# Identity products in TensorE's rests, a convolution that starts before the last stores have landed, and weight splits spread over it: one decoder layer on one core

## The chip, the cores and the metric

The kernel runs on one core of a Trainium2 chip. A core has five engines with queues of their own: TensorE (PE, the matrix products; PEld is its loading of the stationary operand), VectorE (DVE), ScalarE (ACT), GpSimd (POOL) and SyncE (SP, which here issues all the DMAs). They meet by semaphores. The metric is the time of one execution on the device in microseconds (us); lower is better.

## The reference

One layer of a decoder on 16 sequences of 512 tokens with 256 features, all in fp32. Three parts, each followed by a residual sum and a layernorm:

```python
x = _layernorm(x + _L0_attn_ref(x, ...))      # a gated long convolution, then a gated MLP of 672
x = _layernorm(x + _L0_xattn_ref(x, ctx_512, ...))   # causal attention, 16 heads, plus attention to 64 context rows
x = _layernorm(x + _L0_ffn_ref(x, ...))       # low-rank MLP 256 -> 64 -> 1024 -> 64 -> 256 with GELU

# in _L0_attn_ref:
z = rmsnorm(u, pre_norm_w) @ in_proj_w.T                # 768 channels
z_pre = conv_general_dilated(zc, short_w, ...) + short_b[None, :, None]      # 3 taps per channel
x2, x1, v = jnp.split(z_pre, 3, axis=1)
h = jnp.sum(residues[:, :, None] * jnp.exp(log_poles * t[None, None, :]), axis=1)
xv = x1 * v
yconv = irfft(rfft(xv, n=n) * rfft(h, n=n)[None], n=n)[..., :Lc]    # causal convolution, 512 long
y = (yconv + xv * D_skip[None, :, None]) * x2
y = y.transpose(0, 2, 1) @ out_proj_w.T + u
zm = rmsnorm(y, post_norm_w)
return y + jax.nn.gelu(zm @ l1_w.T) * (zm @ l2_w.T) @ l3_w.T
```

## The kernel before

The program is five stages, each a `Block` in which every engine has its own list. A block ends with a barrier of all engines, so the next stage's first instruction on any engine comes after the last of this one on every engine. Loops over the 16 sequences (`over`, `over_late`) write out the first and last steps and loop over the rest.

- **project** (`pj_` tiles, lines 230 to 526): per sequence, rmsnorm, transpose on TensorE (`turn`, L452), six products of 128 channels (`products3`, L125 to L127), the taps on ScalarE and VectorE. SyncE's `store` writes the gate `x2` to memory (`gate_d`, L284) when tap 0 is done and then the chunks of `xv` into the resident tile `xv_all` (L287) when they are transposed. At the end SyncE waits for all these stores; then a second small block (`Names.clear`, L102 to L108) clears the stage's 28 semaphores.
- **longconv** (`lv_`, 529 to 671): the convolution by chunks of 32, as a scan over chunk states. 32 pairs of channel groups, all written out. Per pair GpSimd builds three small filter tiles, TensorE runs `gather` for the pair after next (L613), the products inside a chunk (L627) and those that leave a state (L634); VectorE scans the states (L663), and ScalarE copies the result back into `xv_all` (L582, L585). TensorE's products of a pair wait until ScalarE has copied the pair before last. In the pairs of the table `WEIGHTS` ScalarE also makes the rounded high halves of the MLP's five weights (`weight_high`) and VectorE, a pair later, the low halves (`weight_low`).
- **mlp** (`ml_`, 674 to 1030): per sequence the output projection (`out_product`), rmsnorm, transpose (`turn`, L932), gate and up products, GELU, the down product (`down`). A product in fp32 precision is made of three products of rounded halves, so `products3` is the unit everywhere.
- **attend** (`at_`, 1096 to 1734): a hand-written table of slots (`SLOTS`) fixes for each engine which job stands where. Jobs t0 and t1 transpose x, q and k project queries and keys, whose parts go to memory and back (`parts_d`), y and p at the end transpose and project the result. The first two steps (b = -2 and -1) only fill the pipeline, and `TAIL` empties it.
- **ffn** (`ff_`, 1758 to 2025): `turn` (L1828), `first`, `hidden` (L1842, L1843), `second` (L1850), `last_product`.

## Time and profile before

| | us |
|---|---|
| runs | 2195.28, 2195.38, 2197.44 |
| median | 2195.38 |
| the profiled execution | 2197.36, of which 2195.6 span |
| TensorE busy | 1985.4 (90% of the span) |
| VectorE, ScalarE, GpSimd busy | 1468.2, 1222.3, 883.2 |
| mean granted clock of TensorE | 0.965 |

The stages lie one behind another in the span: project until 217, longconv until 287, mlp until 784, attend until 1977, ffn to the end. The granted clock is given as a share of 2.4 GHz; it has two levels, 1.00 and 0.50 (1.2 GHz), and a value between is a mean over a stretch with both. A row of the timeline gives the start, the duration and the count of instructions that follow each other, and in brackets how long the engine had been idle and which engine's work ended that.

### The profile page before, as it was taken

What the parts mean: (1) busy time and instruction counts of PE and PEld (TensorE: products, weight loads), DVE (VectorE), ACT (ScalarE), POOL (GpSimd) and SP (SyncE); (2) the same over time, 40 slices, a digit from 0 to 9 for tenths busy, and PEclk for the clock granted to TensorE, in tenths of its full rate; (3) what the DMA queues carried; (4) which work ended last, traced back from release to release, by engine and by line L of the source; (5) the groups of instructions that cost most, each with busy time, mean ns of one, the idle gap of its engine ahead of it and who ended that gap; (6) DMA issues with size and microseconds to landing.
All of it is one profiled execution on the core that took longest, in us unless ns stands there. A gap on an engine that the chain in (4) does not pass through costs nothing. (4 is left out here: it accounts for less than half of the span.)

```text
span 2195.6 us, 39396 instructions
## 1 busy us (share of the span) xinstructions
PE 1985.4 (90%) x12897; PEld 1348.4 (61%) x12960; DVE 1468.2 (67%) x2652; ACT 1222.3 (56%) x2425; POOL 883.2 (40%) x1336
## 2 busy tenths in 40 slices
PE   6786949999999868999999999999999999968997
PEld 4665337888888755566566665566655665535554
DVE  6898634555555427777778777777777787724776
ACT  6775535555555423665656656565656556645554
POOL 3443615555555431334333434344333433332222
PEclk9999969999999979999999999999999999978999
DMA  3343121211122244343443344342443334112221
GB/s 116 123 149 125 44 77 68 77 68 69 67 73 76 78 106 91 77 106 72 104 105 85 79 93 103 92 103 64 109 103 80 90 81 94 43 39 66 78 87 66
DMA packets 104787, 188.10 MB, mean 86 GB/s; under 512 B 27961, under 2 KB 78137, under 8 KB 98489
## 3 DMA queue, kind: packets, MB, share of 16 engines
q1 hardware_dynamic: 104632, 186.13, 31.7%
q8 instruction: 86, 1.41, 0.3%
q14 instruction: 69, 0.56, 0.1%
HBM read 110.23 MB, written 58.79 MB: 77 GB/s over the span
## 5 line engine op out<-in xcount | busy, mean ns | idle before, releaser
L1516 ACT ACTIVATE at_pt<-at_ps_w 128x512 f32<-128x512 f32 x640 | 377.8, 598 | 232.8 <-PE at_ps_w L1392 232.7
L1743 DVE TENSOR_REDUCE at_mneg<-at_ps_s 128x1 f32<-128x384 f32 (+3 forms) x704 | 437.3, 636 | 94.9 <-PE at_ps_s L1381 87.3
L1606 POOL TENSOR_SCALAR_AFFINE_SELECT at_pt<-at_pt 128x256 f32<-128x256 f32 (+1 forms) x640 | 233.5, 368 | 576.3 <-ACT at_pt L1516 573.8
L1380 PE MATMUL at_ps_s<-at_ks,at_qs 96*128 96x128 bf16 (+3 forms) x1024 | 259.4, 306 | 25.0 <-DVE at_mneg L1743 22.7
L1392 PE MATMUL at_ps_w<-at_qs,at_ks 97*128 97x512 bf16 (+3 forms) x1024 | 244.3, 301 | 9.0 <-ACT at_pt L1516 5.0
L1380 PEld LDWEIGHTS at_ps_s<-at_ks,at_qs 96*128 96x128 bf16 x1024 | 86.2, 99 | 215.1 <-DVE at_mneg L1743 140.5
L895 POOL TENSOR_TENSOR ml_m_lo<-ml_m,ml_m_hi 128x512 fp32r<-128x512 f32 x80 | 115.9, 1450 | 181.0 <-ACT ml_m_hi L801 180.7
L1408 PE MATMUL at_ps_o<-at_pt,at_val 128*32 128x512 f32 (+3 forms) x2048 | 169.1, 449 | 9.7 <-POOL at_pt L1606 9.5
L1381 PE MATMUL at_ps_s<-at_mask,at_ident 128*128 128x128 bf16 (+1 forms) x641 | 149.4, 233 | 0.0
L834 ACT ACTIVATE ml_gl<-ml_ps_g 128x512 f32<-128x512 f32 x96 | 56.7, 591 | 153.8 <-PE ml_ps_u L127 150.0
L1392 PEld LDWEIGHTS at_ps_w<-at_qs,at_ks 97*128 97x128 bf16 x1024 | 88.3, 98 | 62.9 <-ACT at_pt L1516 14.8
L1559 POOL TENSOR_TENSOR at_parts<-at_rest,at_parts 128x512 bf16<-128x512 f32 x64 | 74.4, 1163 | 130.4 <-ACT at_parts L1493 130.4
L125 PE MATMUL ml_ps_o<-gw_wd,ml_m_hi 128*128 128x256 f32 x320 | 91.8, 287 | 12.8 <-POOL ml_rest L900 7.0
L1022 DVE TENSOR_TENSOR ml_m<-ml_gl,ml_ps_u 128x512 f32<-128x512 f32 x80 | 54.7, 683 | 72.7 <-POOL ml_rest L900 42.0
L381 ACT ACTIVATE pj_zc<-pj_ps_z,pj_tb,pj_tap 128x512 f32<-128x512 f32 x96 | 74.5, 780 | 47.0 <-PE pj_ps_z L127 46.9
L1666 DVE TENSOR_REDUCE at_mcneg<-at_ps_j 128x8 f32<-128x512 f32 x128 | 87.7, 685 | 17.3 <-PE at_ps_j L127 17.2
L1911 ACT ACTIVATE ff_hid<-ff_ps_h,fw_bias 128x512 f32<-128x512 f32 x128 | 79.3, 687 | 35.5 <-PE ff_ps_h L1843 34.2
L1669 DVE TENSOR_TENSOR at_sd<-at_ps_j,at_mcneg 128x512 f32<-128x512 f32 x128 | 88.6, 692 | 13.5 <-DVE at_mcneg L1666 0.5
L1002 DVE TENSOR_TENSOR ml_r<-ml_ps_o,ml_xy 128x1024 f32<-128x1024 f32 x16 | 19.6, 1225 | 116.3 <-PE ml_ps_o L943 116.3
L125 PE MATMUL at_ps_j<-at_x_hi,ea_w_hi 128*128 128x512 f32 x192 | 90.8, 473 | 6.7 <-DVE at_rest L1647 5.2
L125 PE MATMUL pj_ps_z<-pj_x_hi,pj_w_hi 128*128 128x512 f32 x192 | 80.2, 418 | 15.2 <-DVE pj_x_lo L483 15.2
L1408 PEld LDWEIGHTS at_ps_o<-at_pt,at_val 128*32 128x32 f32 x2048 | 51.9, 111 | 66.3 <-issue 44.3
(255 smaller groups left out, 5582.3 us busy)
## 6 DMA issues: line engine op xcount, KB each, us to landing
parts_d<-at_parts SPq DMA_DIRECT2D x64, 384.0 KB, 2.5
at_ks<-parts_d SPq DMA_DIRECT2D x192, 128.0 KB, 7.8
at_qs<-parts_d SPq DMA_DIRECT2D x32, 384.0 KB, 5.7
pj_xin<-in_x SPq DMA_DIRECT2D x16, 512.0 KB, 5.3
gate_d<-pj_zc SPq DMA_DIRECT2D x16, 512.0 KB, 2.7
xv_all<-pj_turned_xv SPq DMA_DIRECT2D x16, 512.0 KB, 4.2
ml_turned_y<-xv_all SPq DMA_DIRECT2D x16, 512.0 KB, 3.4
ml_x<-gate_d SPq DMA_DIRECT2D x16, 512.0 KB, 4.3
```

The lines of the kernel that those rows point to most:

```text
L125: pe.matmul(out, lh, rh, start=first and k == 0, stop=False)
L895: pool.tensor_tensor(m_lo[slot(k, par)][:], m[k % 2][:], m_hi[slot(k, par)][:].bitcast(F32), ALU.subtract).then_inc(m_low, 1)
L1380: pe.matmul(out[:, i, :], qs[par][0:ROWS, h, toks], ks[par][0:ROWS, h, 0:(qt + 1) * P], start=i == 0, stop=False)
L1381: pe.matmul(out[:, :, toks], ident16[:], mask16[:, 0:count, :], start=False, stop=True).then_inc(scored, 1)
L1392: mm = pe.matmul(bank[:, at0:at0 + T - kt * P], ks[par][:, h, kt * P:(kt + 1) * P], qs[par][:, h, kt * P:T], start=True, stop=True)
L1408: mm = pe.matmul(ps_o[j * VW:(j + 1) * VW, kt * P:T], val[par][:, kt, g * HG + j, :], pt[unit % RING][:, at0:at0 + T - kt * P], start=kt = ...
L1516: act.activation(pt[u % RING][:], ps_w[u % 2][:], ACT.Exp, scale=SCALE).then_inc(exped, 1)
L1606: pool.affine_select(out=diag, in_=diag, compare_op=ALU.is_ge, fill=0.0, base=0, pattern=pattern, channel_multiplier=-1).then_inc(cut, 1)
L1666: dve.tensor_reduce(top, scored_c, AX_X, ALU.max, negate=True).then_inc(mc_set, 1)
L1669: dve.tensor_tensor(sd[qt][:].rearrange("p (e s) -> p e s", s=CL), scored_c, top.unsqueeze(2).to_broadcast([P, HE, CL]), ALU.add).then_inc ...
L1743: dve.tensor_reduce(mneg[:, g, h0 % HG:h0 % HG + count, qt], view_score(ps_s[s % 2], qt, count), AX_X, ALU.max, negate=True).then_inc(maxe ...
L1911: act.activation(hid[k % RING][:], ps_h[k % RING][:], ACT.Gelu_apprx_tanh, bias=bias1[:, k:k + 1]).then_inc(gelu_done, 1)
```

## The change

Four edits.

1. **The end of the project stage.** Its semaphores live on (`held`) until the convolution is over. Its block ends without waiting for the stores. In longconv TensorE waits for the `xv_all` stores before its first gather, and SyncE for the `gate_d` stores before it loads weights into the same memory. The clearing block is gone: SyncE clears the 28 semaphores inside longconv, behind its loads. The 7 semaphores of longconv (`spent`) are cleared by SyncE at the end of mlp. In `store` the `xv_all` store now comes ahead of the `gate_d` store.
2. **The weight splits** are cut into eight pieces, the high halves on ScalarE in pairs 8 to 15, the low halves on VectorE in pairs 12, 14 to 26, where before all lay in pairs 28 to 31.
3. **Identity products** (`keep_running`): the 128x128 identity times itself, in fp32, into a PSUM region that nobody reads then, so many in a row: 24 at the end of project; 42, 24 and 8 around the first `out_product` and `turn` of mlp; 24 and 32 around the last `down`; 6 and 16 behind jobs t1 and k0 in step -2 of attend; 5 and 5 ahead of y0 and p0 in its tail and 30 at its end; 6 and 6 behind the first two transposes of ffn. They wait for nothing. (A further place, behind job r3 in the last step, never comes up, since that job isn't in that step.)
4. Whatever the loops held is unchanged.

```diff
-    def clear(self):
-
-        with self.nc.Block() as block:
-            @block.sync
-            def _(sp):
-                for semaphore in self.semaphores:
-                    sp.sem_clear(semaphore)
+    def of(self, name):
+
+        return next(s for s in self.semaphores if s.name == f"{self.tag}_{name}")
...
+def keep_running(pe, out, square, count):
+
+    for _ in range(count):
+        pe.matmul(out, square, square, start=True, stop=True)
...
             def store(b, par):
+                sp.wait_ge(chunked, KT * (b + 1))
+                sp.dma_start(xv_all[:, bass.ds(b, 1)].rearrange("p o g n -> p (o g n)"),
+                             turned_xv[par][:].rearrange("p g n -> p (g n)")).then_inc(placed[par], 16)
                 sp.wait_ge(tap0_done, CT * (b + 1))
                 sp.dma_start(x2_d[bass.ds(b, 1)].rearrange("o p k t -> (o p) k t"),
                              zc[par][:, 0:KT, :]).then_inc(x2_stored[par], 16)
-                sp.wait_ge(chunked, KT * (b + 1))
-                sp.dma_start(xv_all[:, bass.ds(b, 1)].rearrange("p o g n -> p (o g n)"),
-                             turned_xv[par][:].rearrange("p g n -> p (g n)")).then_inc(placed[par], 16)
...
-            for i in range(2):
-                sp.wait_ge(x2_stored[i], 16 * (B // 2))
-                sp.wait_ge(placed[i], 16 * (B // 2))
             sp.wait_ge(f.filt_in, 16 * C)
...
             over_late(pe, B, step)
+            keep_running(pe, ps_t[:, 0, 0:P], ident[:], 24)
...
-        WEIGHTS = {NP - 4: (0, 1), NP - 3: (2, 3), NP - 2: (4,)}
+        PIECES = [(0, None), (1, 0), (1, 1), (2, 0), (2, 1), (3, 0), (3, 1), (4, None)]
+        HIGH_AT = {8 + i: piece for i, piece in enumerate(PIECES)}
+        LOW_AT = {12 + 2 * i: piece for i, piece in enumerate(PIECES)}
...
         def _(sp):
+            for i in range(2):
+                sp.wait_ge(held.of(f"x2_stored{i}"), 16 * (B // 2))
             for k, w in enumerate((w_out, w_gate, w_up, w_tail, w_down)):
                 sp.dma_start(raws[k][:], w).then_inc(gw.w_loaded[k], 16)
             sp.dma_start(gw.ident[:], c_ident).then_inc(gw.par_loaded, 16)
             sp.dma_start(gw.wsc[:], w_scale).then_inc(gw.par_loaded, 16)
+            sp.wait_ge(gathered, 1)
+            for semaphore in held.semaphores:
+                sp.sem_clear(semaphore)
...
-                if isinstance(p, int):
-                    for k in WEIGHTS.get(p, ()):
-                        weight_high(k)
+                if p in HIGH_AT:
+                    weight_high(*HIGH_AT[p])
...
+            for i in range(2):
+                pe.wait_ge(held.of(f"placed{i}"), 16 * (B // 2))
             gather(0, 0)
             gather(1, 1)
...
-                if isinstance(p, int):
-                    for k in WEIGHTS.get(p - 1, ()):
-                        weight_low(k)
+                if p in LOW_AT:
+                    weight_low(*LOW_AT[p])
...
             store(B - 1)
+            for semaphore in spent:
+                sp.sem_clear(semaphore)
...
+            keep_running(pe, ps_g[1][:, 0:P], ident[:], 42)
             out_product(0)
+            keep_running(pe, ps_g[1][:, 0:P], ident[:], 24)
             turn(0)
+            keep_running(pe, ps_g[1][:, 0:P], ident[:], 8)
...
             over(pe, B, step)
+            keep_running(pe, ps_u[1][:, 0:P], ident[:], 24)
             down(B - 1, 1)
+            keep_running(pe, ps_u[1][:, 0:P], ident[:], 32)
...
                         job(name, of_batch(name, b), 1 - par)
+                        if b == -2 and name in RAMP:
+                            keep_running(pe, ps_o[:, 0:P], ident[:], RAMP[name])
...
+                if name in ("y0", "p0"):
+                    keep_running(pe, ps_s[0][:, 0:P], ident[:], 5)
                 job(name, B - 1, 1)
+            keep_running(pe, ps_s[0][:, 0:P], ident[:], 30)
...
+RAMP = {"t1": 6, "k0": 16, "k1": 0}
...
             for k in range(KT):
                 turn(0, 0, k)
+                keep_running(pe, ps_o[:, 0, 0:P], ident[:], 6)
```

SyncE, the last stores of the project stage and the start of longconv (lc_ and gw_ tiles are filters and MLP weights). Before:

```order
77 L284 DMA gate_d<-pj_zc 128x1024
78 L287 DMA xv_all<-pj_turned_xv 128x1024
79 L238 UNCONDITIONAL_BRANCH
80 L105 UNCONDITIONAL_BRANCH
81 L108 ISA x28
82 L104 UNCONDITIONAL_BRANCH
83 L561 UNCONDITIONAL_BRANCH
84 L564 DMA lv_raw_o<-in_w_out 128x512
85 L564 DMA lv_raw_g<-in_w_gate 128x1280
```

After:

```order
77 L285 DMA xv_all<-pj_turned_xv 128x1024
78 L288 DMA gate_d<-pj_zc 128x1024
79 L240 UNCONDITIONAL_BRANCH
80 L562 UNCONDITIONAL_BRANCH
81 L567 DMA lv_raw_o<-in_w_out 128x512
82 L567 DMA lv_raw_g<-in_w_gate 128x1280
...
87 L569 DMA gw_wsc<-in_post_w 128x2
88 L572 ISA x28
```

The two stores have changed places, and the 28 semaphore clears (ISA) stand behind the loads instead of in a block between the stages.

ScalarE in longconv, the rows with the high halves (gw_). Before, in pairs 28 and 29:

```order
152 L585 ACTIVATE xv_all<-lv_ps_y 64x16x16 x2
153 L578 ACTIVATE gw_wo<-lv_raw_o 128x512
154 L576 ACTIVATE gw_wg<-lv_raw_g,gw_wsc 128x640 x2
155 L582 ACTIVATE xv_all<-lv_ps_y 128x16x16
156 L585 ACTIVATE xv_all<-lv_ps_y 64x16x16 x2
157 L576 ACTIVATE gw_wu<-lv_raw_u,gw_wsc 128x640 x2
158 L576 ACTIVATE gw_wt<-lv_raw_t,gw_wsc 128x128 x2
```

After, in pairs 8 to 10:

```order
112 L590 ACTIVATE xv_all<-lv_ps_y 64x16x16 x2
113 L580 ACTIVATE gw_wo<-lv_raw_o 128x512
114 L587 ACTIVATE xv_all<-lv_ps_y 128x16x16
115 L590 ACTIVATE xv_all<-lv_ps_y 64x16x16 x2
116 L583 ACTIVATE gw_wg<-lv_raw_g,gw_wsc 128x640
117 L587 ACTIVATE xv_all<-lv_ps_y 128x16x16
118 L590 ACTIVATE xv_all<-lv_ps_y 64x16x16 x2
119 L583 ACTIVATE gw_wg<-lv_raw_g,gw_wsc 128x640
```

One piece now stands behind the copies of each of eight pairs, the first twenty pairs earlier than before.

TensorE at the joint of longconv and mlp, then at the first transposes of mlp. After (before, L634 was followed at once by the ml_ps_o products, and the ml_ps_t transposes stood alone):

```order
412 L640 MATMUL lv_ps_y<-lv_state,lv_leave 128x256 x2
413 L533 UNCONDITIONAL_BRANCH
414 L920 UNCONDITIONAL_BRANCH
415 L130 MATMUL ml_ps_g<-gw_ident 128x128 x42
416 L121 MATMUL ml_ps_o<-gw_wo,ml_y_hi 128x256
417 L122 MATMUL ml_ps_o<-gw_wo,ml_y_lo 128x256
418 L123 MATMUL ml_ps_o<-gw_wo,ml_y_hi 128x256
...
439 L123 MATMUL ml_ps_o<-gw_wo,ml_y_hi 128x256
440 L130 MATMUL ml_ps_g<-gw_ident 128x128 x24
441 L939 MATMUL ml_ps_t<-gw_ident,ml_yn 128x128 x8
442 L130 MATMUL ml_ps_g<-gw_ident 128x128 x8
443 L121 MATMUL ml_ps_g<-ml_t_hi,gw_wg 128x512
```

The L130 rows are the identity products; they stand ahead of whatever the next row waits for.

## Rows read from the trace of the kernel before

**Rows 1.** TensorE by stretch: stretch, length, busy (instructions), granted clock, DMA share, GB/s.

```profile
206.30:217.00 10.70, 0.00 (x0) 0.72 0.26 101
218.00:221.40 3.40, 3.26 (x18) 0.50 0.80 282
224.60:276.00 51.40, 51.40 (x458) 1.00 0.02 7
297.50:303.00 5.50, 5.42 (x24) 0.50 0.00 0
770.60:776.10 5.50, 5.39 (x45) 0.99 0.01 3
1956.30:1968.70 12.40, 8.80 (x50) 0.50 0.00 0
1977.90:1993.70 15.80, 11.27 (x34) 0.53 0.17 63
```

**Rows 2.** Timeline, end of project, start of longconv, with the landing (DMA issues) fourth.

```profile
208.82 1.90 DVE L504 STREAM_TRANSPOSE pj_turned_xv<-pj_xv 128x512 f32<-128x512 f32 x2
211.67 0.55 SPq L287 DMA_DIRECT2D xv_all<-pj_turned_xv  x1
217.66 0.35 SPq L564 DMA_DIRECT2D lv_raw_o<-in_w_out  x1
xv_all<-pj_turned_xv SPq DMA_DIRECT2D x1, 512.0 KB, 3.5
218.14 2.24 PE L613 MATMUL lv_ps_u<-xv_all,lv_enter 128*64 128x256 f32 x8 [11.85 <-POOL lv_enter L596]
```

**Rows 3.** Timeline, the last pairs of longconv: TensorE, ScalarE, the next stage on GpSimd.

```profile
274.01 0.70 PE L634 MATMUL lv_ps_y<-lv_state,lv_leave 64*128 64x256 f32 x4
275.82 0.70 PE L634 MATMUL lv_ps_y<-lv_state,lv_leave 64*128 64x256 f32 x4
280.98 1.23 PE L634 MATMUL lv_ps_y<-lv_state,lv_leave 64*128 64x256 f32 x4 [3.86 <-DVE lv_state L667]
276.54 1.53 ACT L576 ACTIVATE gw_wg<-lv_raw_g,gw_wsc 128x640 fp32r<-128x640 f32 x2
283.49 1.48 ACT L578 ACTIVATE gw_wd<-lv_raw_d 128x1536 fp32r<-128x1536 f32 x1
285.91 0.78 ACT L585 ACTIVATE xv_all<-lv_ps_y 64x256 f32<-64x256 f32 x2
287.23 0.10 POOL L853 MEMSET ml_mhalf<- 128x4 f32 x1 [13.09 <-POOLq L534]
```

**Rows 4.** Timeline of TensorE: transposes in project, then the start of mlp.

```profile
22.27 1.10 PE L452 MATMUL pj_ps_t<-pj_ident,pj_xn 128*128 128x128 f32 x8 [1.02 <-ACT pj_xn L345]
297.58 0.55 PE L125 MATMUL ml_ps_o<-gw_wo,ml_y_hi 128*128 128x256 f32 x1 [12.15 <-POOL ml_y_lo L859]
309.33 1.97 PE L932 MATMUL ml_ps_t<-gw_ident,ml_yn 128*128 128x128 f32 x8 [6.29 <-ACT ml_yn L814]
313.68 0.80 PE L125 MATMUL ml_ps_g<-ml_t_hi,gw_wg 128*128 128x512 f32 x1 [2.37 <-DVE ml_t_lo L996]
```

**Rows 5.** Timeline, end of mlp and start of attend: TensorE, then ScalarE.

```profile
766.15 0.58 PE L125 MATMUL ml_ps_o<-gw_wd,ml_m_hi 128*128 128x256 f32 x1 [7.01 <-POOL ml_rest L900]
784.12 1.94 PE L1315 MATMUL at_ps_j<-ea_ident,ea_xin 128*128 128x128 f32 x8 [8.13 <-PEq L676]
787.57 0.76 PE L125 MATMUL at_ps_j<-at_x_hi,ea_w_hi 128*128 128x512 f32 x1 [1.50 <-DVE at_x_lo L1633]
796.63 0.69 ACT L1469 ACTIVATE at_parts<-at_ps_j,ea_bias 128x512 bf16<-128x512 f32 x1 [1.97 <-DMA parts_d<-at_parts]
```

**Rows 6.** Timeline of TensorE: end of attend, start of ffn.

```profile
1962.35 1.94 PE L1361 MATMUL at_ps_j<-ea_ident,at_y 128*128 128x128 f32 x8 [1.36 <-DVE at_y L1710]
1977.95 1.09 PE L1828 MATMUL ff_ps_t<-fw_ident,fw_xin 128*128 128x128 f32 x4 [7.78 <-PEq L1099]
1992.77 1.08 PE L1850 MATMUL ff_ps_q<-ff_hid,fw_raw_u 128*64 128x512 f32 x4
```

More of the change, by code:

```diff
@@ L231, in project @@
             f, lp_rows, lp_cols, res_cols, lp_chan, res_chan, skip, c_left, c_ramp, c_lag, c_qmask, c_hmask, c_gmask, c_notfirst,
-            filt_d):
+            filt_d, held):
     CT = 3 * KT
@@ L526, in _, with longconv @@
             over_late(dve, B, step)
-def longconv(nc, f, xv_all, gw, w_out, w_gate, w_up, w_tail, w_down, w_scale, c_ident):
+def longconv(nc, f, xv_all, gw, w_out, w_gate, w_up, w_tail, w_down, w_scale, c_ident, held):
     NP = G // 2
@@ L667, in step, with mlp @@
                 dve.memset(state[par][:, 0:W].rearrange("p (b c) -> p b c", c=NC)[:, :, 0:1], 0.0).then_inc(restarted, 1)
-                if isinstance(p, int):
-                    for k in WEIGHTS.get(p - 1, ()):
-                        weight_low(k)
+                if p in LOW_AT:
+                    weight_low(*LOW_AT[p])
             over_pairs(dve, step)
-def mlp(nc, x, x2_d, gw, xv_all, x1_d, early, c_ident, c_heads, w_qkcv, w_ctx, w_proj, b_qkc, b_ck, b_rows, ctx_t):
+    return n.semaphores
+def mlp(nc, spent, x, x2_d, gw, xv_all, x1_d, early, c_ident, c_heads, w_qkcv, w_ctx, w_proj, b_qkc, b_ck, b_rows, ctx_t):
     with ExitStack() as ctx:
@@ L1430, in step @@
                         job(name, of_batch(name, b), 1 - par)
+                        if b == -2 and name in RAMP:
+                            keep_running(pe, ps_o[:, 0:P], ident[:], RAMP[name])
+                        if is_last(b) and name in ("r3",):
+                            keep_running(pe, ps_s[0][:, 0:P], ident[:], 6)
                     if back(b) and u - LAG in LAST_UNIT:
@@ L2043, in decoder_layer @@
                     f = Filters(nc, filters)
+                    held = Names(nc, filters, "pj")
                     project(nc, a["x"], a["w_in"], a["pre_w"], a["taps"], a["tap_bias"], a["c_ident"], xv_all, gate_d,
                             f, a["lp_rows"], a["lp_cols"], a["res_cols"], a["lp_chan"], a["res_chan"], a["skip"], a["c_left"],
-                            a["c_ramp"], a["c_lag"], a["c_qmask"], a["c_hmask"], a["c_gmask"], a["c_notfirst"], filt_d)
+                            a["c_ramp"], a["c_lag"], a["c_qmask"], a["c_hmask"], a["c_gmask"], a["c_notfirst"], filt_d, held)
                     gw = GatedWeights(nc, gated)
-                    longconv(nc, f, xv_all, gw, a["w_out"], a["w_gate"], a["w_up"], a["w_tail"], a["w_down"], a["post_w"], a["c_ident"])
-                mlp(nc, a["x"], gate_d, gw, xv_all, x1_d, early, a["c_ident"], a["c_heads"], a["w_qkcv"], a["w_ctx"], a["w_proj"],
+                    spent = longconv(nc, f, xv_all, gw, a["w_out"], a["w_gate"], a["w_up"], a["w_tail"], a["w_down"], a["post_w"], a["c_ident"], held)
+                mlp(nc, spent, a["x"], gate_d, gw, xv_all, x1_d, early, a["c_ident"], a["c_heads"], a["w_qkcv"], a["w_ctx"], a["w_proj"],
                     a["b_qkc"], a["b_ck"], a["b_rows"], a["ctx_t"])
```

39 lines of the change are left out of this document (18 added, 21 removed).

## The prediction

> **What bounds the kernel now.** I read the stretches of TensorE first [rows 1]. In the long middles of the stages its busy time is the stretch itself, at a granted clock of 1.00, the 2.4 GHz level (51.40 of 51.40 us in the convolution). Nothing in the change shortens those. What is left is the joints between the stages: stretches in which TensorE rests for 1.5 to 12 us, and behind each rest a stretch at 0.50, the 1.2 GHz level, in which 24 products took 5.42 us where 45 of the same shape took 5.39 us at 0.99. So 128x256 products cost 0.226 and 0.12 us, and a joint costs twice: the rest, and the slow restart. The change works on both, so each joint is costed alone, and whether the saved time reaches the end is asked there: every stage starts at a barrier of all engines, so what a joint saves moves all that follows.
>
> **Part 1, the convolution begun early.** Now the last transposes of VectorE end at 210.72, SyncE issues gate_d and then, at 211.67, xv_all, which lands 3.5 us later, at 215.2; then come the barrier, 28 semaphore clears, a second barrier, SyncE's first load of the next stage at 217.66 and the first product of the convolution at 218.14 [rows 2]. After: xv_all is issued first, at about 210.8, the barrier falls near 212.3, and TensorE alone waits for the landing. By 3.5 us that is 214.3, by the fuller issue behind it perhaps 215: between 3.1 and 3.9 us saved, taken as 3.9, since the store now goes ahead of gate_d and shares the engines less. GpSimd's first filter tiles are built in that wait. The 24 identity products behind the project stage end near 211.5 and still leave 3 us of rest, so the clock probably falls again; the old rest of 10.70 us had a mean of 0.72. The start now runs at 0.50 from 218.0 and at 1.00 from 224.6 on [rows 1], so some 6.4 us of products take twice their time: 3 us. I take 1.2 us of it back (0 to 3 by where the fall comes).
> The weight loads wait for the gate_d stores, go out about 3 us earlier than now, and their first reader is 8 pairs (14 us) further on: nothing.
>
> **Part 2, the weight splits spread.** A pair of the convolution lasts 1.81 us (274.01 to 275.82) [rows 3]. Behind pair 29 TensorE stood still for 3.86 us, resumed at half clock, waited again, and the next stage began at 287.23. Without splits there, pairs 30 and 31 follow at once (they have no gathers, so 1.2 us each): last product ends at 279.0, ScalarE copies until 280.3 (0.78 us for two of three copies, 1.2 for all), next stage at about 280.6: 6.65 us saved. The price is in the pairs where the pieces go. ScalarE's copies take 1.2 us of 1.81 and a gate or up piece 0.77 (half of 1.53), so it falls behind by 0.12 us in each of four pairs, makes it up on the small tail pieces, and falls behind by 0.85 on the down piece of 1.48 us. TensorE needs a pair's copies only two pairs later, which by the starts is 0.47 us of slack; I charge 0.4 us. VectorE's state is asked for by TensorE a pair after VectorE may compute it, and a piece (by ScalarE's, an estimated 0.8 us, the last some 1.5 to 2) comes only in every second pair: nothing. Net 6.25 us (5.3 to 6.7).
>
> **Part 3, the identity products.** An identity product is 128x128 by 128 in fp32. The trace of before has no such row. The nearest is the transposes of the same shape, eight in 1.10 us at full clock and in 1.94 to 1.97 at half [rows 4], so 0.11 and 0.21 us an instruction. The other fp32 products that are not transposes have two instructions each in the trace. So one costs 0.21 us warm, 0.43 cold. From below 0.1 us, if it were one instruction; from above the cold price. Each count then fits its rest at full clock and only there:
> - Start of the MLP stage: 42 x 0.21 = 9.0 us in a rest of 12.15 us (10.3 of it behind the barrier); 24 x 0.21 = 5.1 in 6.29; 8 x 0.21 = 1.7 in 2.37 [rows 4]. Gain: the 24 output products, 5.42 - 24 x 0.12 = 2.5, taken as 2.4, and the eight transposes, 0.85. The gate and up products behind them get faster too, but the next output product waits for GpSimd's chain, so nothing more. 3.2 us.
> - End of the MLP stage: 24 (5.1 us) in 7.01 [rows 5]; some 20 down products speed up by 0.105: 2.0 us. The stage now also clears 7 semaphores behind its last store; the 28 of part 1 fit between 215.2 and 217.66 with two barriers, some 0.06 each: -0.4. Net 1.6 us.
> - Start of attention: 32 (6.8 us) in 8.13 less barrier; 6 (1.3) in 1.50 [rows 5]. The path is transposes, copies, first query projection: 0.6 us on the transposes (half of them hide behind the copies) and six 128x512 products at twice 0.105, 1.2 us. Then 16 more (3.4 us) stand before the second query projection. That one's reader, ScalarE at 796.63, waits for a store of parts [rows 5], so by my count the projection is in time to 0.1 us. 1.75 us (0.5 to 2).
> - End of attention: 5 products before each of two steps. Here TensorE has been at 0.50 for all of 12.40 us [rows 1], so they may cost 2.1 us each against a rest of 1.36 us [rows 6]: 0.8 and 0.7 us lost if the clock stays down, 0.6 won if it rises one step earlier. Zero (-1.5 to +1).
> - Start of the feed-forward: 30 (6.4 us) in 7.78 less barrier [rows 6], 6 and 6 (1.3) in two rests in which ScalarE and VectorE split a half, as in the 1.50 us at the start of attention [rows 5]. Of the 15.80 us at 0.53, 11.27 were busy, so 5.6 is the most to be had. Two sets of four transposes (0.85) and six products (1.2) are surely on the path; of the eight hidden products and transposes behind them, ScalarE's table load and two GELUs let about half through before 1992.77. 3.4 us (2.0 to 4.5).
>
> These lean on the clock being held by identity products. Row by row: plain fp32 products held 1.00 for 51.40 us of convolution [rows 1], and they are of this kind. Against it stands the stretch at 1956.3, where transposes, small products and rests gave 8.80 us busy of 12.40 and the clock never rose [rows 1].
> The Trainium skill, "TensorE: Matmul & The Clock Gate", Part 4: PE-mode transpose, says that transpose-mode work does not engage the full clock. The new products multiply the identity with itself as plain products, so the rule would not cover them; if it did, the sum would be that of the slower rival below. The trace of before does not decide it.
>
> **The sum.** 3.9 + 1.2 + 6.25 + 3.2 + 1.6 + 1.75 + 0 + 3.4 = 21.3 us. The profiled execution took 2197.36 us (span 2195.6); the median of the three runs is 2195.38, 2.0 us lower. The two levels differ probably by where the clock fell in such joints, which the change evens out, so I credit half: 2197.36 - 21.3 - 1.0 = 2175.0 us.
>
> **Rivals.**
> A. *The rests stay too long, and the clock falls in what is left of them.* Each filling stops 0.5 to 1.5 us short of the next work, and at the end of attention the clock stayed at half over a rest of only 1.36 us [rows 6]. Then parts 1 and 2 stand (3.9 + 6.25), and of part 3's 10 us perhaps a quarter: 12.7 us, 2183.7. For it: the stretch at 1956.3 was 71% busy and never rose [rows 1]. Against it: after the fillings TensorE is busy for over four fifths of those stretches.
> B. *Identity products do not hold the clock* (the slower one). Each then costs 0.43 us. The overrun over the rests: 42 gives 17.9 - 10.3 = 7.6; 24 gives 3.9; 8 gives 1.0; 24 gives 3.2; 32 runs past the barrier by 6.4; 6 by 1.0; 16 by 3.4; 5 and 5 by 1.5; 30 by 5.7; 6 and 6 by 2.2: 36 us. Less the 10.2 of parts 1 and 2, some 2221 us. It decides at the point where the clock is gone before the filling ends. This is what the page's rule would give if it held for plain products too.
> C. *The convolution does not profit as counted*: weight pieces on ScalarE stall TensorE pair after pair, or the stage still starts late because the xv_all store lands no sooner. Its worst: 1.3 us for five pieces with no slack and 3 us of part 1 gone, 2179.
>
> **How the numbers follow.** Forecast 0.76, A 0.14, B 0.04, C 0.06. The bounds of the single terms, independent of each other, add to about -5 and +5 us; A and C lie within +9. So 2169.5 to 2182.5, which leaves out B and the worst of A. A measurement of this kernel tells about 0.2% (4.4 us) from no change: all but B lie more than that below 2195.38. Faster 0.94, same 0.02 (A and C together with the worst bounds), slower 0.04.
>
> **What would show it.** Right: the first product of the convolution 3 to 4 us earlier; no wait of TensorE for a VectorE state behind pair 28, and the stage's end 6 us nearer to its start; output products of the first batch 0.12 us apart, at clock 1.00; the first 128x512 products of attention and feed-forward 0.23 us apart. Wrong: identity products 0.2 us or more apart per instruction, a barrier that TensorE reaches last, the second query projection's reader waiting for TensorE, or a granted clock of 0.50 right behind a filling.

## The result, and the profile after

The changed kernel took 2180.57 us (median of 5 runs, 2173.32 to 2184.31), the kernel before 2195.38: a ratio of 0.9923, 95% interval 0.9897 to 0.9949. Measured twice more, beside the experiments, it took 2178.26 against 2198.22 us (0.9907, 0.9889 to 0.9924) and 2175.76 against 2195.84 us (0.9905, 0.9889 to 0.9921). The forecast was 2175.0, in a range of 2169.5 to 2182.5. So the gain is some 15 to 20 us where 20.4 was said. The single times spread over 11 us, and the first profiled execution was the slowest of its five: 2184.31 us, span 2182.3.

Page of the changed kernel, part 2, 40 slices (busy tenths of TensorE, then the granted clock in tenths). Only two slices of the clock still stand below 9, and these are shares of stretches in which it fell:

```profile
PE   6888979999999978999999999999999999989997
PEclk9999999999999989999999999999999999979999
```

The project stage's end and the convolution's start, timeline of the changed kernel (start, length, engine, line, operation, and in brackets the rest ahead of it and who ended it). They answer to [rows 2]:

```profile
209.74 5.52 PE L130 MATMUL pj_ps_t<-pj_ident 128*128 128x128 f32 x48
212.43 1.94 DVE L503 STREAM_TRANSPOSE pj_turned_xv<-pj_xv 128x512 f32<-128x512 f32 x2
214.41 0.56 SPq L285 DMA_DIRECT2D xv_all<-pj_turned_xv  x1
215.01 0.58 SPq L288 DMA_DIRECT2D gate_d<-pj_zc  x1
217.49 1.98 PE L617 MATMUL lv_ps_u<-xv_all,lv_enter 128*64 128x256 f32 x8 [2.22 <-DMA xv_all<-pj_turned_xv]
```

L130 is the identity product: 24 of them are 48 instructions in 5.52 us, 0.115 each, and 0.23 a product, where 0.21 had been taken. From VectorE's last transposes to the first product of the convolution it is now 5.06 us; it was 9.32 [rows 2]. TensorE waits for the landing of xv_all alone, 3.08 us behind its issue.

The convolution's end and the start of the MLP stage, against [rows 3, 4]:

```profile
277.17 0.70 PE L640 MATMUL lv_ps_y<-lv_state,lv_leave 64*128 64x256 f32 x4
279.59 9.62 PE L130 MATMUL ml_ps_g<-gw_ident 128*128 128x128 f32 x84 [1.72 <-PEq L533]
291.01 0.39 PE L121 MATMUL ml_ps_o<-gw_wo,ml_y_hi 128*128 128x256 f32 x1 [1.80 <-POOL ml_y_lo L866]
292.41 0.34 PE L123 MATMUL ml_ps_o<-gw_wo,ml_y_hi 128*128 128x256 f32 x1
292.55 0.41 PE L121 MATMUL ml_ps_o<-gw_wo,ml_y_hi 128*128 128x256 f32 x1
```

The wait of 3.86 us for a VectorE state is gone, and the last pairs follow at once. The identity products end at 289.21, 1.80 us ahead of the first output product. These begin at full clock and lose it at 292.5, though TensorE has not paused since 291.01. Windows of TensorE (stretch, length, busy, clock, DMA share, GB/s) show it beside the places where the clock held, against [rows 1]:

```profile
217.50:220.90 3.40, 3.40 (x20) 0.51 0.54 168
291.00:292.50 1.50, 1.49 (x12) 0.99 0.00 0
292.50:295.10 2.60, 2.60 (x14) 0.50 0.00 0
757.40:765.20 7.80, 7.73 (x65) 1.00 0.16 62
777.00:783.40 6.40, 6.40 (x45) 1.00 0.06 20
1945.50:1959.00 13.50, 12.21 (x70) 0.53 0.01 1
1960.00:1966.80 6.80, 6.80 (x64) 1.00 0.00 0
1970.40:1975.60 5.20, 3.62 (x23) 1.00 0.33 101
```

The end of the MLP stage and the starts of attention and of the feed-forward run at 1.00. The end of attention runs at half clock as before, from 1945.5 until about 1958, and its identity products with it. The rest of 3.21 us ahead of it is where the clock goes: the 2 us ahead of 1945.5 have a mean of 0.75.

**Where the time went, segment by segment.** Each segment ends at an event that both kernels have, so the gains add up to the difference of the spans. The three columns of gains are the three profiles of the changed kernel (spans 2182.3, 2176.2 and 2177.0), against the one of before:

| from, to | before | predicted gain | first | second | third |
|---|---|---|---|---|---|
| start, VectorE's last transposes in project | 208.82 | 0 | -3.61 | -0.43 | -2.19 |
| to the first product of the convolution | 9.32 | 3.9 | 4.26 | 4.25 | 4.27 |
| to the MLP stage's first load | 69.08 | 7.45 | 7.17 | 7.05 | 8.67 |
| to the first output product | 10.36 | 0 | -1.25 | -1.24 | -0.83 |
| to the first transposes | 11.75 | 2.4 | 1.15 | 2.36 | 2.49 |
| to the first gate product | 4.35 | 0.85 | 0.88 | 0.88 | 0.88 |
| to the last batch's down products | 452.47 | 0 | 0.08 | 0.26 | 0.08 |
| to attention's first transposes | 17.97 | 1.6 | 1.31 | 1.33 | 1.31 |
| to its second batch's transposes | 29.06 | 1.75 | 0.97 | 0.85 | 1.03 |
| to the last attention outputs | 1143.19 | 0 | -0.11 | 1.66 | 0.44 |
| to the feed-forward's first transposes | 21.58 | 0 | -1.07 | -1.15 | -1.09 |
| to the end | 217.65 | 3.4 | 3.52 | 3.58 | 3.54 |
| sum | 2195.6 | 21.3 | 13.3 | 19.4 | 18.6 |

Rows that the change touches agree within 0.2 us in the three profiles, but for three: the convolution and the two rows behind it that end at the first transposes. The column of before is a single profile too. Part 1 alone and part 2 alone (below), which have no identity products, took 11.12 and 11.24 us to the first transposes of the MLP stage (11.75 here), 30.50 and 29.59 us to attention's second batch (29.06), and 22.61 and 21.58 us to the feed-forward's first transposes (21.58). So the gains of these three rows are known to some 0.5 to 1.4 us only.

What moved the profiles apart is mostly the first row, in whose loop nothing that TensorE computes was changed. TensorE's windows there, the changed kernel's first profile, then the kernel before:

```profile
36.00:48.00 12.00, 10.63 (x40) 0.86 0.22 67
48.00:60.00 12.00, 10.91 (x44) 0.86 0.36 120
```

```profile
36.00:48.00 12.00, 9.19 (x41) 1.00 0.33 116
48.00:60.00 12.00, 9.26 (x42) 1.00 0.33 115
```

The same steps, with the same rests of 2.04 to 2.70 us ahead of the transposes of batches 2 to 5, lost the clock in one profile and kept it in the other (which lost it once, between 60 and 72). A step of batches 2 to 5 took 12.5 to 13.2 us where the clock stayed up, and up to 14.8 us where it fell. Over the eleven profiles whose project stage has no fillings inside, the sum of five such steps goes with the time at half clock in the first 208 us: 64.4 to 64.5 us with 3.4 us of it (three profiles), 65.9 with 6.8 to 6.9 (two), 66.7 to 67.5 with about 10.2 (five), 67.8 with 13.7 (one).

### The profile page after: what moved, and what is told of

Read it like the earlier page. It is cut to its first block and busy times, and to the rows that moved or that the text cites. A ratio compares the mean times of both kernels' runs of the same rounds, so it can differ in the third digit from the quotient of the medians.

```text
span 2182.3 us, 40306 instructions
## 1 busy us (share of the span) xinstructions
PE 2025.3 (93%) x13353; PEld 1392.7 (64%) x13416; DVE 1467.5 (67%) x2652; ACT 1222.7 (56%) x2425; POOL 883.6 (40%) x1336
## 5 line engine op out<-in xcount | busy, mean ns | idle before, releaser
L1685 DVE TENSOR_REDUCE at_mcneg<-at_ps_j 128x8 f32<-128x512 f32 x128 | 87.6, 684 | 17.1 <-PE at_ps_j L123 16.9
L121 PE MATMUL pj_ps_z<-pj_x_hi,pj_w_hi 128*128 128x512 f32 x192 | 81.8, 426 | 13.7 <-DVE pj_x_lo L482 13.7
```

The source lines that it names most:

```text
L121: pe.matmul(out, lh, rh, start=first and k == 0, stop=False)
L1685: dve.tensor_reduce(top, scored_c, AX_X, ALU.max, negate=True).then_inc(mc_set, 1)
```

## Experiments

All eleven runs were timed in five rounds beside the kernel before.

**Each part alone.** Part 1 is the held semaphores, the moved waits and the order of the stores. Part 2 is the spread splits. Part 3 is all identity products and nothing else.

```
+            for i in range(2):
+                pe.wait_ge(held.of(f"placed{i}"), 16 * (B // 2))
             gather(0, 0)
```

> Part 1 alone: the kernel before with the convolution begun early (and the stores in their new order), without the spread splits and without identity products. In the changed kernel's profile the first product of the convolution starts 5.06 us behind VectorE's last transposes of the project stage, where it was 9.32 us. Theory (the terms of the prediction hold alone): 5.0 to 5.3 us there, and 4 to 5 us off the median. In that profile the project stage itself, whose work is the same, was 3.61 us longer (last transposes at 212.43 instead of 208.82). Theory: that is where TensorE's clock happened to fall in the rests of the first batches, so here it lands anywhere from 207 to 213. Rival (the new order of the stores, gate_d behind xv_all, slows the stage): 212 to 213 again, and no gain over 1.5 us in the median.

Measured: 2190.23 against 2198.64 us (0.9964, 0.9951 to 0.9977), 8 us, where 4 to 5 were said. VectorE's last transposes to the first product: 4.99 us, as said. The convolution itself also took 67.49 us instead of 69.08, which the expectation left out: the clock was back at 1.00 some 3.2 us behind its first product, where it had taken 6.4. The two together are 5.9 us, inside the interval of 5 to 11. VectorE's last transposes came at 210.31. With the old order of the stores they came at 211.23 (part 2 alone) and 210.97 (part 3 alone), so the rival with the stores falls.

```
-        WEIGHTS = {NP - 4: (0, 1), NP - 3: (2, 3), NP - 2: (4,)}
+        HIGH_AT = {8 + i: piece for i, piece in enumerate(PIECES)}
+        LOW_AT = {12 + 2 * i: piece for i, piece in enumerate(PIECES)}
```

> Part 2 alone: the kernel before with the weight splits spread over pairs 8 to 26. Theory: from the first product of the convolution to the first load of the next stage 62.5 to 63 us (69.08 before, 61.91 in the changed kernel, of which up to 1 us is the clock at the start, which is not changed here), so 6.2 to 6.6 us off the median. Rival (the pieces stall TensorE in their pairs and the early start hid it): over 64 us. The first output product of the MLP stage came 11.61 us behind that first load in the changed kernel and 10.36 before; if the spread splits or the nearer end of the convolution did that, it is 11.6 here, if it is the identity products or chance, 10.4.

Measured: 2192.27 us (0.9974, 0.9961 to 0.9986), 6 us. The convolution took 63.30 us, just over the 62.5 to 63 that were said, so 5.78 us are won. From its first product to pair 29 it took 58.37 us where it had taken 57.68: the pieces cost 0.69 us, not 0.4. The first output product came 10.31 us behind the first load: the loss there isn't from this part.

```
+            keep_running(pe, ps_g[1][:, 0:P], ident[:], 42)
             out_product(0)
+            keep_running(pe, ps_g[1][:, 0:P], ident[:], 24)
...
```

> Part 3 alone: the kernel before with all its identity products. Prediction: 10 us (3.2 at the start of the MLP stage, 1.6 + 0.4 at its end, 1.75 at the start of attention, 0 at its end, 3.4 at the start of the feed-forward). By the changed kernel's profile the terms are nearer to 1.15 + 0.9, 1.3, 1.0, -1.1 and 3.5, so 6 to 7 us off the median. Rival for the 1.25 us that the first output product of the MLP stage lost: 11.6 us behind the stage's first load here too, if TensorE's identity products delay the loads or the engines ahead of it; 10.4 if not. Identity products at 0.115 us an instruction at full clock in all places but the end of attention, where they run at 0.23.

Measured: 2189.81 us (0.996, 0.9945 to 0.9975), 9 us, where 6 to 7 were expected (the interval is 5.5 to 12). The three parts alone add to 22 us; their intervals are about 3 us wide to each side, so this does not differ from the 18 to 20 us of the whole. The output products to the transposes took 9.37 us, 2.38 us less than before, as predicted (1.8 less than in part 1 alone and part 2 alone), and the first output product came 11.99 us behind the first load. Here the loss is. It has two causes. Windows of TensorE, part 3 alone:

```profile
289.30:294.30 5.00, 5.00 (x24) 0.50 0.81 272
294.30:301.00 6.70, 6.70 (x61) 1.00 0.52 191
```

The 84 instructions began at half clock, took 12.0 us instead of 9.6, and ended behind the operand they wait for. And the loads were late. DMA of the 13 us behind the stage's first load (KB, and the median us to landing), in part 3 alone and in part 2 alone:

```profile
q8 instruction: 1, 0.02, 0.6%
ml_turned_y<-xv_all SPq DMA_DIRECT2D x2, 512.0 KB, 3.6
ml_x<-gate_d SPq DMA_DIRECT2D x2, 512.0 KB, 4.7
ml_xin<-in_x SPq DMA_DIRECT2D x1, 512.0 KB, 6.8
```

```profile
ml_turned_y<-xv_all SPq DMA_DIRECT2D x2, 512.0 KB, 3.2
ml_x<-gate_d SPq DMA_DIRECT2D x2, 512.0 KB, 4.0
ml_xin<-in_x SPq DMA_DIRECT2D x1, 512.0 KB, 5.3
```

An instruction load of 0.02 MB went out between the data. Over all 13 profiles of this study it fell 1 to 4 us behind the first load in six (the changed kernel's three, part 3 alone, and the kernels below on the end of attention and on the convolution's two ends), and ml_xin landed after 6.2 to 6.8 us in all six. In six others it fell before that load, more than 10 us behind it or not near it at all, and ml_xin landed after 5.1 to 5.4 us. In one it fell at 6 us, between the two (5.3, with ml_x at 4.3). Of the ten profiles with part 3, the first output product waited for the late operand in three (11.60 to 12.19 us behind the first load), stood right behind a filling that had begun at half clock in five (11.00 to 11.99), and came at 10.32 and 10.26 us in the two that are left.

**The project stage's rests filled.**

```
                     if k == 2 and not is_last(b):
+                        if isinstance(b, int) and 1 <= b <= 3:
+                            keep_running(pe, ps_t[:, 0, 0:P], ident[:], 8)
                         turn(b + 1, 1 - par)
```

> The changed kernel with eight more identity products (1.84 us at full clock) in each of the three long rests of the project stage, ahead of the transposes for batches 2, 3 and 4, which waited 2.19, 2.04 and 2.70 us for ScalarE. Theory (the clock falls by chance in these rests; steps there took 12.5 us without a fall and 13.6 to 14.2 with one): steps of 12.5 to 12.8 us, the last transposes of VectorE at 207 to 208.5 (208.82 before, 212.43 in the changed kernel), the single times closer together than the 11 us of the changed kernel, and a median 1.5 to 4 us under its own (2180.57). Rival (the falls come from something else in the stage, or the new products delay the transposes): steps still up to 14 us, and a time as that of the changed kernel or above.

Measured: 2176.15 us (0.9908, 0.9889 to 0.9927). VectorE's last transposes came at 208.28 us, inside the 207 to 208.5 that were said and below all eleven profiles without the filling (208.82 to 212.43). The five steps behind the first took 12.70, 12.52, 13.18, 12.63 and 12.93 us, 63.96 in sum. In the eleven profiles without this filling the sum was 64.35 to 67.75, 66.3 on average; the last kernel below, with it, has 63.76. In this kernel's project stage the clock fell in one place only, at 74 to 78 us, right behind the rest of 2.04 us that was not filled. So the falls in these rests are what lengthens the stage, and filling them takes some 2 us of it away. Two of the five steps stayed above the 12.5 to 12.8 us that were said. The median does not tell the gain: the ratio is that of the changed kernel, and its single times still spread over 8 us.

**The changed kernel again.**

> The changed kernel itself, on the same chip as the next three, as the measure for them. Theory (the 3.61 us that the project stage took longer in its first profile are where the clock fell by chance): the last transposes of VectorE anywhere from 208 to 213 us, and the median near 2180 or 18 us under the kernel before. Theory on the 1.25 us that the first output product of the MLP stage lost (an instruction load of 0.02 MB fell into the loads of the first batch in that profile and in that of part 3 alone, and into none of the profiles where those loads took their old time): 10.4 us behind the first load where none falls into it, 11.6 to 12.0 us where one does.

Measured as said: project to 209.25, first output product at 11.60 us with an instruction load 3 us behind the first load. With the same rest ahead of the output products as in the first profile (1.81 us) the clock did not fall this time: 9.39 us to the transposes.

**Transposes for products.**

```
-    for _ in range(count):
-        pe.matmul(out, square, square, start=True, stop=True)
+    for _ in range(-(-5 * count // 3)):
+        pe.transpose(out, square, square)
```

> The changed kernel with TensorE transposes of the identity in place of the identity products, five for every three, since eight transposes took 1.09 us at full clock (0.136 each) where a product takes 0.23. So each filling lasts as long as before, if the clock holds. Theory (any back-to-back work of TensorE holds the clock): within 3 us of the changed kernel. Rival (the Trainium skill, TensorE: Matmul & The Clock Gate, Part 4: transpose-mode work does not engage the full clock): the clock falls within the long fillings, transposes there take 0.24 us each (eight in 1.94), each filling runs on past its rest, the first output product of the MLP stage comes 15 us or more behind the first load instead of 10.4 to 11.6, and the time is above the kernel before.

Measured: 2180.64 us (0.9927, 0.9913 to 0.994), no more than 3 us from the changed kernel. Windows of TensorE at the start of the MLP stage (the transposes run from 276.54 to 286.04) and in the filling between attention and feed-forward:

```profile
276.50:278.50 2.00, 1.96 (x10) 0.54 0.48 193
278.50:280.50 2.00, 2.00 (x13) 0.60 1.00 315
280.50:286.00 5.50, 5.50 (x51) 1.00 0.81 280
1953.00:1958.00 5.00, 5.00 (x49) 1.00 0.00 0
```

In the first filling nothing but transposes ran, the clock rose under them from 0.50 to 1.00, and it stayed there. The Trainium skill, "TensorE: Matmul & The Clock Gate", Part 4, says that the full clock does not engage for transpose-mode work; for these transposes of fp32 128x128 tiles the measurement says otherwise, and it decides.

**The end of attention.**

```
                 g, c = CHUNKS[k]
+                if is_last(b) and k == NCH - 1:
+                    keep_running(pe, ps_s[0][:, 0:P], ident[:], 12)
```

> The changed kernel with twelve more identity products (2.76 us at full clock) in the rest of 3.21 us ahead of the last attention outputs, behind which all of the end of attention ran at 0.50. Theory (term G failed because the clock had fallen ahead of the fives; they hold a clock that is there but do not bring it back in time): the 24 output products start at 1.00 and take 1.50 us instead of 2.79, the ten identity instructions 1.15 instead of 2.34 and 2.50, and from the last outputs to the first transposes of the feed-forward stage it takes 19 to 20.5 us instead of 22.65; 2 to 3 us off the time. Rival (that stretch waits for the other engines): 22 us and no gain; or the clock falls in spite of it.

(Term G is the two sets of five at the end of attention.) Measured: 2176.85 us (0.99, 0.9885 to 0.9916). TensorE in the changed kernel, then with the twelve:

```profile
1945.52 2.79 PE L1420 MATMUL at_ps_o<-at_pt,at_val 128*32 128x384 f32 x24 [3.21 <-POOL at_pt L1625]
1949.93 2.34 PE L130 MATMUL at_ps_s<-ea_ident 128*128 128x128 f32 x10
1954.54 2.50 PE L130 MATMUL at_ps_s<-ea_ident 128*128 128x128 f32 x10 [0.56 <-DVE at_yt_lo L1702]
```

```profile
1941.84 2.84 PE L130 MATMUL at_ps_s<-ea_ident 128*128 128x128 f32 x24
1945.22 1.50 PE L1422 MATMUL at_ps_o<-at_pt,at_val 128*32 128x384 f32 x24 [0.54 <-POOL at_pt L1627]
1947.93 1.28 PE L130 MATMUL at_ps_s<-ea_ident 128*128 128x128 f32 x10
1951.43 1.38 PE L130 MATMUL at_ps_s<-ea_ident 128*128 128x128 f32 x10 [0.98 <-DVE at_yt_lo L1704]
```

From the last outputs to the feed-forward's first transposes it now takes 18.13 us instead of 22.65, 4.5 us less and more than expected, so the rival that this stretch waits for the other engines falls. Against the three profiles with the same fives in which the clock came back early (20.72 to 21.00 us, see below on the end of attention) it is 2.6 to 2.9 us. The clock had fallen in the rest of 3.2 us in all eleven profiles without the twelve, and stayed up in both with them. In the median little of it shows, since this profile's steady part of attention was the longest of all (1145.58 us), with the clock at 0.50 in several stretches between 790 and 838 and from 1920 to 1930.

**The convolution's two ends.**

```
+            keep_running(pe, ps_u[0][:, 0:P], square, 6)
             for i in range(2):
                 pe.wait_ge(held.of(f"placed{i}"), 16 * (B // 2))
...
             over_pairs(pe, step)
+            keep_running(pe, ps_u[0][:, 0:P], square, 5)
```

> The changed kernel with identity-like products in three more rests: six ahead of the convolution's first wait for xv_all, five behind the last product of the convolution, and 44 instead of 42 at the start of the MLP stage (the first two sets multiply a filter tile with itself). Theory (what is left of rests of 1.7 to 2.2 us is enough to lose the clock): first products of the convolution at 1.00, from the first one to the next stage's first load 60.3 to 61 us instead of 61.91; the 24 output products of the first batch at 1.00 throughout (2.9 us from the first to the last start instead of 3.9); 1.5 to 3 us off the time. Rival (TensorE reaches the barrier last, or the fillings overrun): 62 us or more, or the first output product right behind the last identity product and later than 11.6 us.

Measured: 2178.35 us (0.9905, 0.989 to 0.992), the same as the changed kernel. The first products, with the six ahead of them:

```profile
215.15 1.57 PE L130 MATMUL lv_ps_u<-lc_toep 128*128 128x128 f32 x12 [0.87 <-PEq L240]
216.65 1.08 PE L617 MATMUL lv_ps_u<-xv_all,lv_enter 128*64 128x256 f32 x8
```

They took 1.08 instead of 1.98 us, the convolution 60.43 instead of 61.91 us, and all 24 output products ran at full clock. But the changed kernel's third profile shows the same without any filling, behind the same rest of 2.22 us as in the first:

```profile
216.06 1.08 PE L617 MATMUL lv_ps_u<-xv_all,lv_enter 128*64 128x256 f32 x8 [2.22 <-DMA xv_all<-pj_turned_xv]
```

Of seven profiles with both parts and a rest there (2.22 to 2.26 us, in one 3.24), two kept the clock (60.41 and 60.52 us) and five lost it at the start or in the first products (61.91 to 62.03); both with the filling kept it. The MLP stage's first filling began at full clock in both, and at half clock in six of the eight others with part 3. The first output product still came late here (12.19 us), with an instruction load 1 us behind the first load.

**Wide products at the start of the MLP stage.**

```
-            keep_running(pe, ps_g[1][:, 0:P], ident[:], 42)
+            keep_running_wide(pe, ps_g[1], ident[:], 11)
```

> The changed kernel with the 42 identity products at the start of the MLP stage made as 11 products four times as wide (128x128 by 128x512, the identity repeated), so 22 instructions instead of 84 for the same 9.6 us. Theory (the instruction load that falls into the first batch's loads is TensorE's own, for the added instructions): no instruction load within 13 us of the stage's first load, ml_x lands after 4.0 us instead of 4.7 and ml_xin after 5.2 instead of 6.8, and the first output product comes 10.3 to 10.5 us behind the first load instead of 11.6, 1.2 us off the time. Rival (the loads are slowed by something else): 11.6 us as now.

Measured: 2178.08 us (0.9918, 0.9905 to 0.9931). The instruction load was not gone, but fell 11 us behind the first load, and the loads landed after 3.2, 3.8 and 5.1 us, as expected. The gain was then lost to the other cause: the 22 instructions began at half clock, took 11.38 us, and the first output product came right behind them, at 11.00 us. So the lateness of the loads goes where the instruction load goes. That the 84 narrow instructions bring it there isn't shown: the kernel with the project filling has them too, its instruction loads fell 1 us ahead of the first load and 13 us behind it, and its ml_xin landed after 5.2 us.

**All together**, with 22 more products in the rest ahead of attention's second batch.

```
+                        if b == -1 and name == "t0":
+                            keep_running(pe, ps_o[:, 0:P], ident[:], 22)
                         job(name, of_batch(name, b), 1 - par)
```

> The changed kernel with all that helped so far: eight more identity products in each of three rests of the project stage; six ahead of and five behind the convolution; wide products at the start of the MLP stage; twelve ahead of the last attention outputs; and, new, 22 (5.06 us) in the rest of 5.4 to 6.9 us in which TensorE waits for the second batch's x at the start of attention, behind which it ran at 0.50 for about 12 us. By the segments: 0.5 to 2 off the project stage, 1.5 off the convolution, 1.3 off the MLP start, 1 to 3 off attention's start, 2 to 4.5 off its end: 7 to 11 us under the changed kernel, 2167 to 2171, if each place keeps its gain. Rival (the clock falls elsewhere instead, and the mean stays): within 3 us of the changed kernel, 2175 to 2181.

> The changed kernel once more, as the measure for these two, and for the spread of its segments: theory (chance decides where the clock falls in the project stage, in the attention stage's steady part and nowhere else): the project stage between 208 and 213, from the second batch's transposes in attention to the last outputs 1139 to 1146 us, all other segments within 0.3 us of the profile before.

Measured: 2167.89 us (2166.30 to 2168.62) against 2175.76 of the changed kernel and 2195.84 of the kernel before on the same chip: 0.9871 of the latter (0.9857 to 0.9886), and 7.9 us under the former, whose interval (0.9889 to 0.9921) it does not touch. Its timeline, at the MLP start and at attention's second batch:

```profile
274.56 9.68 PE L136 MATMUL ml_ps_g<-gw_ident 128*128 128x512 f32 x22 [0.45 <-PEq L542]
284.63 0.39 PE L121 MATMUL ml_ps_o<-gw_wo,ml_y_hi 128*128 128x256 f32 x1 [0.39 <-POOL ml_y_lo L878]
788.81 5.07 PE L130 MATMUL at_ps_o<-ea_ident 128*128 128x128 f32 x44
```

Its segments against the changed kernel's three profiles: VectorE's last transposes in project 208.74 (209.25 to 212.43), the convolution 60.45 (60.41 to 62.03), to the first output product 10.26 (11.19 to 11.61), attention's first batch 27.38 (28.03 to 28.21), its steady part 1138.28 (1141.53 to 1143.30), its end 18.20 (22.65 to 22.73). The start of attention gave less than the 1 to 3 us that were said. The 22 products kept the clock up for 24 us behind them, of which the twelve other profiles spend 6.8 to 14.5 us at half clock; what part of the shorter steady part is theirs isn't shown, since the kernel with the project filling has 1139.23 without them. The four single times now lie within 2.3 us of each other. The changed kernel's third profile missed its expectation in one place, the convolution (60.41 us).

## Why the prediction was right, and where not

**Part 1, right.** 3.9 us were taken and 4.25 to 4.27 measured in every profile with it: xv_all landed 3.1 us behind its issue, not 3.5. The clock at the start of the convolution (1.2 us taken, 0 to 3 as bounds) is one of two outcomes: against part 2 alone (63.30 us) about 1.4 us where it fell and 2.9 where it did not.

**Part 2, right, mis-sized by half a microsecond.** 6.25 taken, 5.78 measured. 0.3 of it is ScalarE's pieces in the pairs, 0.69 us for 0.4.

**Part 3.** That plain identity products hold the clock and fill a rest for about their counted time is shown in every place where the clock was there when they began. Term by term:
- Start of the MLP stage, 3.2 us: the two gains came as counted against the one profile of before (2.4 and 0.88) where the clock held, but 0.8 to 1.25 us were lost ahead of them. The step that failed is the prediction's "Each count then fits its rest at full clock and only there". It had no term for the rest of 1.7 us behind the barrier, after which the products may begin at half clock (11.24 us instead of 9.62, in the third profile), nor for loads that land later than in the old trace (the first two profiles).
- End of the MLP stage, 1.6: measured 1.3. Part 3 alone gave 2.02, as counted. With the semaphore clears the segment took 16.64 to 16.66 us instead of 15.95, so they seem to cost 0.7, not 0.4 (0.6 between part 1 alone and part 2 alone, 18.90 and 18.30).
- Start of attention, 1.75: measured 0.85 to 1.03, but the term was right and the one profile of before hides it. The chain was counted rightly up to the third of the query projections: from the first transposes to the product at 788.89 below it took 14.76 us instead of 16.45. The second batch's x was issued 17.71 us behind the first transposes instead of 19.56, a gain of 1.85 that is the same in every profile with the plain identity products (17.70 to 17.73; the three without any have 19.56 to 19.57). From issue to use it then took 10.38 us where it had been 9.50 (issued at 803.68, used at 813.18). That is not the change's doing: the three profiles without identity products took 9.50, 10.93 and 10.03 us, the ten with fillings 9.65 to 10.84. Against the mean of the three, 29.72 us, the whole segment gained 1.5 to 1.7. A sign of being wrong did come here, for little: the second query projection's reader, ScalarE at 785.03, waits for TensorE, 2.21 us where it had waited 1.97 for the store.

```profile
788.89 0.47 PE L121 MATMUL at_ps_j<-at_x_hi,ea_w_hi 128*128 128x512 f32 x1 [2.50 <-DVE at_rest L1666]
791.84 0.62 SPq L1220 DMA_DIRECT2D ea_xin<-x_d  x1
802.22 1.94 PE L1327 MATMUL at_ps_j<-ea_ident,ea_xin 128*128 128x128 f32 x8 [6.93 <-DMA ea_xin<-x_d]
```

- End of attention, 0 (-1.5 to +1): measured -1.07 to -1.15. In the second profile the two fives pushed the transposes and the products behind them by 0.56 and 1.24 us (0.8 and 0.7 predicted), and an earlier rise gave 0.66 back (0.6 predicted). The mechanism was right, and so perhaps was zero. Of eight profiles with fives behind a fallen clock, five took 22.65 to 22.73 us, and three (the project filling, the transposes, the convolution's two ends) took 20.72 to 21.00: in these the clock was back before the second five, whose ten instructions (nine in the transposes) took 1.38 to 1.40 us instead of 2.50. The three without fives took 21.58, 21.58 and 22.61; the means are 22.0 and 21.9. So the fives cost 1.1 us or win 0.6 to 0.9, by when the clock comes back, and what decides that stays open.
- Start of the feed-forward, 3.4: measured 3.52 to 3.58.

**The sum.** The touched segments give 16.9, 17.9 and 20.3 us in the three profiles, where the sum had 21.3. The rest of the distance is the first row of the table, which cost 0.4 to 3.6 us in these profiles. The profile of before had been a fast one there, which is luck and no merit of either kernel: 208.82 us, where VectorE's last transposes come at 209.25 to 212.43 in the ten others without the project filling. The sum leaned on that one profile as if every rest outside the changed places were fixed. And the last step, "the two levels differ probably by where the clock fell in such joints, which the change evens out, so I credit half", fails: the change left the project stage's rests as they were, and the changed kernel's times spread over as much as before (11 us).

**The rivals.** A (what is left of the rests loses the clock) is true here and there: behind 1.80 us in the first profile and not behind 1.81 in the second (nor behind 1.94 in the kernel on the convolution's two ends), and at the convolution in five of seven. It was priced at 8.6 us for all places together; it cost 1.5 us at the convolution and 1.2 at the output products, each in some profiles only. B, the slower one, is excluded at every place with the clock up; at the end of attention, where the clock was down before they began, the fives ran at 0.23 to 0.25 us an instruction. C cost 0.3 us.

Of the signs of being right, all came but one: the first output products stood 0.12 us apart for twelve of 24 only, in the first profile. Three signs of being wrong came too, for 0.2 to 1.5 us each: identity products 0.2 us or more apart (the fives; the first filling of the MLP stage in the third profile), the reader that waits for TensorE, and a clock of 0.50 behind a filling (behind the 2.22 us left of the rest at the convolution, and at 292.5).

## What to carry to other kernels

To keep TensorE's clock over a rest, fill it from a point at which the clock is still up, and leave about a microsecond or less: fillings that left 0.1 to 1.1 us kept a clock that was up in every profile here. Longer rests went both ways: 1.65 to 1.71 us behind plain fillings kept it each time, 1.72 to 1.98 us behind the convolution lost it in six profiles of eight. At the end of attention twelve cheap products ahead of the fall were worth 2.6 to 4.6 us, while ten behind it cost 1.1 us in five profiles and won 0.6 to 0.9 in three. Before adding up such gains, compare several profiles segment by segment, of the kernel before as well: a segment in which nothing changed differed by 3.6 us here, largely through the clock, and hides or feigns a part's gain. A single profile of before made one right term look like a miss.

## What the hardware showed that was not expected

Whether the clock falls behind a rest of 1.7 to 2.7 us is not settled by the rest's length: a rest of 2.22 to 2.26 us, behind the same work, was followed by a fall in four profiles and by none in two. What decides stays open. The rest of 3.2 us ahead of the last attention outputs lost the clock in all eleven profiles in which it was left. The fall can also come after the rest is over: at 292.5, after 1.5 us of unbroken products.

TensorE transposes raised the clock from 0.50 to 1.00 by themselves, within 4 us (276.5 to 280.5), and held it.

An instruction load of 0.02 MB, 0.5 to 0.6% of the DMA time around it, went with a landing of a 512 KB load that was 0.8 to 1.7 us later, in six profiles of six. Whether the one delays the other, or both follow from something else, no run here tells.
